# Cross-attention with routed experts: the q product in two halves, in two PSUM banks

## The chip, the cores and the metric

One core of one Trainium2 chip. The metric is the device time of one execution of the kernel in microseconds, the median of several runs. TensorE (PE in the profile) multiplies, VectorE (DVE) and ScalarE (ACT) work on what it leaves in PSUM, GpSimd (POOL) works on SBUF alone, and SyncE (SP) issues most of the transfers. Each engine works through its own instructions in order and waits on semaphores.

## What is computed

The input `x` is 8 batches of 512 tokens of width 512 in float32; with it comes a context of 64 tokens of width 128 for each batch. One layer is computed:

```python
x = x + xattn(layernorm(x), ctx, Wq, Wkv_expand, Wout)
x = x + ffn(layernorm(x), router_w, wg, wu, wd, sg_w, ..., sd_b)

# xattn: 16 heads of 32, a causal mask over the 64 keys
qp = q @ Wq.T
k, v = split(ctx @ Wkv_expand.T)
scores = where(causal, qh @ kh.T / sqrt(32), finfo.min)
out = softmax(scores) @ vh @ Wout.T

# ffn: top 2 of 8 experts by logit (the logit is the weight), and a shared expert
moe = sum over the chosen e of logit[e] * (silu(x @ wg[e]) * (x @ wu[e])) @ wd[e]
out = moe + (silu(x @ sg_w + sg_b) * (x @ su_w + su_b)) @ sd_w + sd_b
```

## The kernel before, in words

A float32 operand of a product is held as two float16 parts, high and low, and a product is three float16 passes (high by high, high by low, low by high; `PASSES`). So every result of PE that feeds another product is read twice out of PSUM: ACT writes the high part (`copy`, L665), and DVE writes what is left as the low part (`low`, L808; L934 for the attention output).

The work has two stages. **The attention stage** takes the 4096 tokens in 32 tiles of 128 (`over_tiles`, L297, calls `step(b, j)` with tile = 4b + j; four tiles make a batch). It is a software pipeline: step `tile` does a different part for each of the tiles t1 = tile - 1 to t5 = tile - 5. **The expert stage** (`entry(n)`) does the shared expert for the 32 tiles and then 71 slots of routed tokens, and begins in the last steps of the attention stage.

What one step does on each engine, in the order in which the engine has it:

- PE (L1276): the q product of t2, 48 matmuls into bank 5 (`turned`, L1267, in the order of the four blocks of 128 output rows); transposes of the attention output of t4 (bank 4), of the probabilities of t3 (banks 0 and 1), of the second norm of t5 (bank 6), and of the first norm `xn1` of t1 (bank 7, L1302 to L1305); the scores of t2 (L1318, 12 matmuls, after a wait for `qT_ready`, into banks 2 and 3); the output projection of t4; the attention product of t3; the router product of t5.
- ACT (L697): logits of t6, the second norm of t5 (L707), the high part of q of t2 (L711), the high parts of attnT, probsT (two), xn2T and xn1T (L725), and in step (0, 2) alone `more_weights` (L727: the high parts of `w_o`, `w_sh`, `w_r`); then the first norm of `tile` (L730), pieces of an expert's weights, and the exponential (L738).
- DVE (L918): the statistics of the first norm of `tile`, a maximum over a third of an expert's weights (L895, not where j = 1), the low part of q of t2 (L929), in step (0, 2) the low part of `w_o` (L931, it waits for `wo_hi` from ACT), the low parts of attnT, probsT (two), xn2T and xn1T, the maximum and the subtraction of the softmax (L955 to L961, L955 where j = 2), the residual (L969) and its statistics, and the attention output (L977, L980). Step (0, 2) ends with `shared_weights`.
- POOL (L558): the power for both norms (L524 to L530), the low parts of the expert's pieces, and where j = 1 four copies of the batch's keys (L545).

`q_mm`, `qT_hi` and `qT_ready` count tiles: one signal of PE, ACT and DVE for each q product. The product of t2 waits for `xn1T_ready` (which also says that bank 7 has been read) and for `qT_ready` of the tile before.

In step (0, 2) PE has one more thing in its order ahead of the transposes of `xn1`: `spread_magnitudes`, which makes the scales of the remaining weights. The weights' high parts on ACT wait for `scales_ready` and stand behind the xn1T copy of that step in ACT's order.

Of the kernel before, what the change touches and what calls it, by code (L numbers as in the profile page):

```python
# [32 lines left out]
P = 128  # L33
B, S, H = 8, 512, 512
# [46 lines left out]
def xattn_moe(nc, x, ctxT, wqT, wkT, wvT, woT, routerT, experts, shared, sh_b, sd_b, out):  # L81
# [5 lines left out]
    with stack:  # L87
# [125 lines left out]
            probsT_flat[:, 0:8 * P], probsT_flat[:, 8 * P:16 * P])]  # L213
        GATE_BANK, UP_BANK, DOWN_BANK, XG_BANK, RANK_BANK, HOT_BANK = (5, 7), (2, 3), (0, 1), (4, 6), 4, 6
        GU_BANK, HT_BANK = GATE_BANK, UP_BANK
        y = w_q[:, :, :].rearrange("p v w -> p (v w)").bitcast(F32).rearrange("p (r w) -> p r w", r=Y_RING)
        attn_flat = attn[:, :, :].rearrange("p h d -> p (h d)")
        y_w = sb("y_w", [P, 4, 1])
# [7 lines left out]
        def flat(t4):  # L226
            return t4.rearrange("p c q -> p (c q)")
# [128 lines left out]
        def _(sp):  # L356
# [55 lines left out]
            def load_shared(n):  # L412

                if n >= 4:
                    sp.wait_ge(up_mm, n - 3)
                else:
                    sp.wait_ge((q_mm, scores_mm, av_mm, av_mm)[n], T)
                sp.wait_ge(xT_stored, 16 * (n + 1))
                sp.dma_start(xgT[n % 4].rearrange("p v c q -> p (v c q)"), xT_dram[n * P:(n + 1) * P, :]
                             ).then_inc(shared_in[n % 4], 16)  # L420
# [242 lines left out]
        def _(act):  # L663
# [33 lines left out]
            def step(b, j):  # L697
                tile = TPB * b + j
                t1, t2, t3, t4, t5, t6 = [tile - n for n in range(1, 7)]
                e, pieces = pieces_at(b, j)  # L700
                if live(t6):
                    act.wait_ge(router_mm, t6 + 1)
                    copy(logits[:, bass.ds(t6, 1), :], psum[:, 6, 0:E], sc[:, S_R:S_R + 1], logits_ready)
                if live(t5):
                    act.wait_ge(ln_rstd[1], t5 + 1)
                    wait(act, xn2_stored[(j + 1) % 2], 16 * (TPB // 2 * b + (j - 5) // 2))
                    act.activation(xn2[:, (j + 1) % 2, 0:H], x1, ACT.Identity, bias=rstd[:, 1, 2:3],  # L707
                                   scale=rstd[:, 1, 1:2]).then_inc(xn2_ready, 1)
                if live(t2):
                    act.wait_ge(q_mm, t2 + 1)  # L710
                    copy(flat(qT[:, 0, :, :]), bank(5), Q_DOWN, qT_hi)  # L711
                if live(t4):
                    act.wait_ge(attnT_mm, t4 + 1)
                    copy(flat(attnT[:, 0, :, :]), bank(4), 1.0, attnT_hi)
                if live(t3):
                    for n in range(2):
                        act.wait_ge(probsT_mm, 2 * t3 + n + 1)
                        copy(probsT_flat[:, 4 * P * n:4 * P * n + 4 * P], bank(n), P_UP, probsT_hi)
                if live(t5):
                    act.wait_ge(xn2T_mm, t5 + 1)  # L720
                    wait(act, xT_stored, 16 * t5)
                    copy(flat(xn2T[:, 0, :, :]), bank(6), X_UP, xn2T_hi)
                if live(t1):
                    act.wait_ge(xn1T_mm, t1 + 1)
                    copy(flat(xn1T[:, 0, :, :]), bank(7), X_UP, xn1T_hi)  # L725
                if isinstance(b, int) and (b, j) == (0, 2):
                    more_weights()  # L727
                if live(tile):
                    act.wait_ge(ln_rstd[0], tile + 1)
                    act.activation(xn1[:, :], x_in[:, j % 2, 0:H], ACT.Identity, bias=rstd[:, 0, 2:3],  # L730
                                   scale=rstd[:, 0, 1:2]).then_inc(xn1_ready, 1)
                if pieces:
                    high_piece(e, pieces[0])
                entry_amid(tile, entry)
                if live(t2):

                    act.wait_ge(shifted, t2 + 1)
                    act.activation(probs[:, :, :], probs[:, :, :], ACT.Exp, scale=sc[:, S_EXP:S_EXP + 1]).then_inc(probs_ready, 1)  # L738
                if len(pieces) > 1:
                    high_piece(e, pieces[1])  # L740
                if isinstance(b, int) and (b, j) == (0, 0):
                    first_weights()
# [34 lines left out]
        def _(dve):  # L777
# [140 lines left out]
            def step(b, j):  # L918
# [6 lines left out]
                if e is not None and j in ((1, 2, 3) if isinstance(b, int) and b == 0 else (0, 2, 3)):  # L925
                    expert_magnitudes(e, max(0, j - 1))
                if live(t2):
                    dve.wait_ge(qT_hi, t2 + 1)
                    low(flat(qT[:, 1, :, :]), bank(5), Q_DOWN, flat(qT[:, 0, :, :]), qT_ready)  # L929
                if isinstance(b, int) and (b, j) == (0, 2):  # L930
                    more_weights()  # L931
                if live(t4):
# [279 lines left out]
        def _(pe):  # L1212
# [63 lines left out]
            def step(b, j):  # L1276
                tile = TPB * b + j
                t1, t2, t3, t4, t5 = [tile - n for n in range(1, 6)]
                if live(t2):

                    pe.wait_ge(xn1T_ready, t2 + 1)
                    wait(pe, qT_ready, t2)
                    if isinstance(t2, int) and t2 == 0:
                        pe.wait_ge(wq_split, 1)
                    turned(bank(5), xn1T, lambda v, c, o: w_q[:, v, c * H + o * P:c * H + (o + 1) * P], C, q_mm)
                if isinstance(b, int) and (b, j) == (0, 2):
                    spread_magnitudes(M_WO, N_MAG)
                if live(t4):
                    pe.wait_ge(attn_ready, t4 + 1)
                    wait(pe, x1_ready, t4)  # L1290
                    transposes(bank(4), attn_flat, C, attnT_mm)
                if live(t3):

                    pe.wait_ge(probs_ready, t3 + 1)
                    wait(pe, attn_ready, t3)
                    for n in range(2):
                        transposes(bank(n), probs_flat[:, 4 * P * n:4 * P * n + 4 * P], PAIRS // 2, probsT_mm)
                if live(t5):
                    pe.wait_ge(xn2_ready, t5 + 1)
                    wait(pe, logits_ready, t5)  # L1300
                    transposes(bank(6), xn2[:, (j + 1) % 2, :], C, xn2T_mm)
                if live(t1):  # L1302
                    pe.wait_ge(xn1_ready, t1 + 1)
                    wait(pe, xn1T_ready, t1)
                    transposes(bank(7), xn1[:, :], C, xn1T_mm)  # L1305
                entry_amid(tile, entry)
                if live(t2):

                    pe.wait_ge(qT_ready, t2 + 1)
                    if isinstance(t2, int) and t2 == 0:  # L1310
                        pe.wait_ge(v_split, 4)
                    wait(pe, shifted, t2)
                    if j == 2:
                        pe.wait_ge(k_bd_ready, HPC * (b + 1))
                    for c in range(C):
                        dst = psum[:, 2 + c // 2, (c % 2) * 2 * P:(c % 2) * 2 * P + 2 * P]
                        for a, z in PASSES:
                            last = pe.matmul(dst, qT[:, a, c, :], k_bd[:, z, c, :, :].rearrange("p h k -> p (h k)"),  # L1318
                                             start=(a == z == 0), stop=(a == 1))
                    last.then_inc(scores_mm, 1)  # L1320
                if live(t4):
                    pe.wait_ge(attnT_ready, t4 + 1)
                    if isinstance(t4, int) and t4 == 0:
                        pe.wait_ge(wo_split, 1)
                    product(bank(4), chunks(attnT), columns(w_o, H), C, proj_mm)
                if live(t3):

                    pe.wait_ge(probsT_ready, 2 * (t3 + 1))
                    if j == 3:
                        pe.wait_ge(v_bd_ready, 2 * (b + 1))  # L1330
                    for r in range(PAIRS):
                        dst = psum[:, r // 4, (r % 4) * 2 * VW:(r % 4 + 1) * 2 * VW]
                        for a, z in PASSES:
                            last = pe.matmul(dst, probsT[:, a, r, :], v_bd[:, z, r, :, :].rearrange("p h w -> p (h w)"),
                                             start=(a == z == 0), stop=(a == 1))
                    last.then_inc(av_mm, 1)
                if live(t5):

                    pe.wait_ge(xn2T_ready, t5 + 1)
                    if isinstance(t5, int) and t5 == 0:  # L1340
                        pe.wait_ge(wsh_split, 3)
                    product(psum[:, 6, 0:E], chunks(xn2T), columns(w_r, E), C, router_mm)
                if isinstance(b, int) and (b, j) == (0, 0):
                    first_products()
# [116 lines left out]
```

## Time and profile before

| | |
|---|---|
| median of 3 runs | 892.38 us |
| the three runs | 892.25, 892.38, 895.52 us |
| the profiled execution, its own time | 895.16 us |
| its span from the first to the last instruction | 893.0 us |
| mean granted TensorE clock | 0.976 |
| busy: PE, DVE, ACT, POOL | 89%, 74%, 46%, 43% of the span |
| chain that ended last | PE 46%, DVE 30%, issue 12%, POOL 5%, ACT 3% |
| attention stage | to about 420 us |

The shares are averages over both stages: PE is what the expert stage runs at, from about 450 us on, and DVE is busiest in the attention stage. The 2.2 us between span and time lie outside the first and last instruction.

### The profile page before, as it was taken

What the parts mean: (1) busy time and instruction counts of PE and PEld (TensorE: products, weight loads), DVE (VectorE), ACT (ScalarE), POOL (GpSimd) and SP (SyncE); (2) the same over time, 40 slices, a digit from 0 to 9 for tenths busy, and PEclk for the clock granted to TensorE, in tenths of its full rate; (3) what the DMA queues carried; (4) which work ended last, traced back from release to release, by engine and by line L of the source; (5) the groups of instructions that cost most, each with busy time, mean ns of one, the idle gap of its engine ahead of it and who ended that gap; (6) DMA issues with size and microseconds to landing.
All of it is one profiled execution on the core that took longest, in us unless ns stands there. A gap on an engine that the chain in (4) does not pass through costs nothing.

```text
span 893.0 us, 22190 instructions
## 1 busy us (share of the span) xinstructions
PE 798.8 (89%) x7484; PEld 541.0 (61%) x7484; DVE 660.2 (74%) x1352; ACT 408.5 (46%) x737; POOL 380.5 (43%) x486
## 2 busy tenths in 40 slices
PE   4559888888898999898999889999999999999994
PEld 1347666767676767676788667645555555555551
DVE  4899999999999999988547887755555555555552
ACT  2345757666666666675532222333333333333330
POOL 1113546454554555553400001046656556656543
PEclk9779999999999999999999999999999999999997
DMA  8215373636363544333576456479989989999892
GB/s 315 97 29 171 107 211 102 192 106 199 104 197 107 164 148 119 105 104 125 185 248 191 143 160 209 135 110 167 147 141 156 148 144 162 148 160 140 147 149 38
DMA packets 102760, 132.39 MB, mean 148 GB/s; under 512 B 54368, under 2 KB 55392, under 8 KB 101280
## 3 DMA queue, kind: packets, MB, share of 16 engines
q1 hardware_dynamic: 86784, 95.74, 37.9%
q0 software_dynamic: 15904, 35.70, 23.2%
q8 instruction: 44, 0.72, 0.4%
q14 instruction: 28, 0.23, 0.1%
HBM read 71.61 MB, written 52.31 MB: 139 GB/s over the span
## 4 chain that ended last, share of the span: by engine, by line
PE 46%; DVE 30%; issue 12%; POOL 5%; ACT 3%; DMA 2%; DVEq 1%; POOLq 1%; SPq 0%; ACTq 0%; another core or an unknown queue 0%
PE psum L1224 33%; PE psum L1272 7%; PE psum L1215 4%; DVE stats L883 4%; DVE head_max L959 3%; DVE probsT L808 3%; DVE xy L969 2%; POOL kv_store L545 2%; DVE xn1T L808 2%; DVE emag L895 1%; DVE qT L808 1%; DMA hidT<-hid_parts 1%; POOL rstd L526 1%; DVE attnT L934 1%; DVE probs L955 1%
## 5 line engine op out<-in xcount | busy, mean ns | idle before, releaser
L645 POOL DMA_INDIRECT out<-w_q,tabs x71 | 112.5, 1584 | 108.7 <-DVE w_q L1203 76.2
L635 POOL DMA_INDIRECT x_in<-normed_tokens,tabs x71 | 71.0, 999 | 147.3 <-DVE tabs L1090 101.1
L1188 DVE SCALAR_TENSOR_TENSOR hid<-psum,tabs,silu_g 128x256 f32<-128x256 f32 x71 | 34.4, 484 | 110.4 <-ACT silu_g L770 108.9
L1224 PE MATMUL psum<-exp_all,hidT 128*128 x426 | 104.5, 382 | 3.2 <-DMA hidT<-hid_parts 3.2
L770 ACT ACTIVATE silu_g<-psum,tabs 128x256 f32<-128x256 f32 x71 | 33.7, 474 | 145.2 <-PE psum L1224 141.1
L1272 PE MATMUL psum<-xn1T,w_q 128*128 128x128 f16 x1536 | 92.6, 221 | 7.5 <-DVE xn1T L808 7.3
L1224 PE MATMUL psum<-exp_all,probsT 128*128 x420 | 96.4, 379 | 0.0
L1272 PEld LDWEIGHTS psum<-xn1T,w_q 128*128 128x128 f16 x1536 | 87.6, 99 | 8.4 <-DVE xn1T L808 8.2
L1224 PE MATMUL psum<-w_o,attnT 128*128 128x512 f16 x384 | 88.9, 381 | 0.0
L524 POOL TENSOR_SCALAR rstd<-moments 128x1 f32<-128x1 f32 x64 | 14.3, 223 | 174.6 <-DVE moments L886 170.8
L738 ACT ACTIVATE probs<-probs,sc 128x1024 f32<-128x1024 f32 x32 | 36.8, 1149 | 84.6 <-DVE probs L961 84.6
L537 POOL TENSOR_TENSOR exp_all<-piece,exp_all 128x512 f32 (+1 forms) x48 | 56.1, 1168 | 44.4 <-ACT piece L665 44.4
L1224 PEld LDWEIGHTS psum<-exp_all,hidT 128*128 128x128 f16 x426 | 41.8, 98 | 54.5 <-issue 5.8
L1318 PE MATMUL psum<-kv_store,qT 128*128 128x256 f16 x384 | 50.5, 284 | 25.4 <-DVE qT L808 24.4
L1203 DVE TENSOR_SCALAR w_q<-psum,y_w 128x512 f32<-128x512 f32 x71 | 53.3, 751 | 22.1 <-PE psum L1224 17.5
L1224 PEld LDWEIGHTS psum<-exp_all,probsT 128*128 128x128 f16 x420 | 41.1, 98 | 41.9
L808 DVE SCALAR_TENSOR_TENSOR probsT<-psum,probsT 128x512 f16<-128x512 f32 x99 | 65.1, 684 | 0.2 <-ACT probsT L665 0.2
L1224 PEld LDWEIGHTS psum<-w_o,attnT 128*128 128x128 f16 x384 | 37.8, 99 | 39.4 <-issue 1.1
L1318 PEld LDWEIGHTS psum<-kv_store,qT 128*128 128x128 f16 x384 | 36.2, 101 | 37.9 <-DVE qT L808 30.6
L665 ACT ACTIVATE probsT<-psum 128x512 f16<-128x512 f32 x99 | 55.6, 599 | 8.0 <-PE psum L1215 7.7
L1224 PE MATMUL psum<-exp_all,xn1T 128*128 x216 | 49.6, 379 | 0.0
L1224 PE MATMUL psum<-exp_all,qT 128*128 x216 | 49.6, 379 | 0.0
(195 smaller groups left out, 1646.1 us busy)
## 6 DMA issues: line engine op xcount, KB each, us to landing
x_in<-x SPq DMA_DIRECT2D x64, 256.0 KB, 2.9
exp_all<-experts SPq DMA_DIRECT2D x8, 1536.0 KB, 7.3
out<-xy SPq DMA_DIRECT2D x32, 256.0 KB, 2.0
normed_tokens<-xn SPq DMA_DIRECT2D x32, 256.0 KB, 2.1
normed_turned<-xn2T SPq DMA_DIRECT2D x32, 256.0 KB, 2.0
w_q<-out SPq DMA_DIRECT2D x32, 256.0 KB, 2.9
out<-w_q SPq DMA_DIRECT2D x32, 256.0 KB, 2.4
probsT<-normed_turned SPq DMA_DIRECT2D x16, 256.0 KB, 3.5
```

The source lines that it names most:

```text
L537: pool.tensor_tensor(split_piece(e, 1, k), piece[:, :], split_piece(e, 0, k), ALU.subtract).then_inc(piece_split, 1)
L635: pool.indirect_dma_start(x_in[:, t % 4, :], None, xn_dram, bass.IndirectOffsetOnAxis(gather_at[:, t:t + 1], 0)).then_inc(gathered[t % 4], 16)
L645: pool.indirect_dma_start(out, bass.IndirectOffsetOnAxis(add_at[:, t:t + 1], 0), y[:, t % Y_RING, :], None, bounds_check=TOKENS - 1, oob_i ...
L665: act.activation(dst, src, ACT.Copy, scale=scale).then_inc(done, 1)
L738: act.activation(probs[:, :, :], probs[:, :, :], ACT.Exp, scale=sc[:, S_EXP:S_EXP + 1]).then_inc(probs_ready, 1)
L808: dve.scalar_tensor_tensor(dst, src, scale, high, ALU.mult, ALU.subtract).then_inc(done, 1)
L883: dve.bn_stats(stats[:, which, :], src).then_inc(ln_chain[which], 1)
L1203: dve.tensor_scalar(y[:, k % Y_RING, :], bank(DOWN_BANK[k % 2]), y_w[:, tk % 4, :], None, ALU.mult).then_inc(y_ready, 1)
L1215: last = pe.transpose(dst[:, c * P:(c + 1) * P], src[:, c * P:(c + 1) * P], ident[:, :])
L1224: last = pe.matmul(dst, lhsT(a, c), rhs(z, c), start=(c == 0 and a == z == 0), stop=(c == n - 1 and a == 1))
L1272: last = pe.matmul(dst[:, o * P:(o + 1) * P], weights(a, c, o), xT[:, z, c, :], start=(c == 0 and a == z == 0), stop=(c == C - 1 and a == 1))
L1318: last = pe.matmul(dst, qT[:, a, c, :], k_bd[:, z, c, :, :].rearrange("p h k -> p (h k)"), start=(a == z == 0), stop=(a == 1))
```

## The change

The q product of a tile is made in two halves of 24 matmuls: output blocks 0 and 1 go to columns 0 to 255 of bank 5, and blocks 2 and 3 to columns 256 to 511 of bank 7. Each half has its own signal, and ACT and DVE each make two instructions of 128x256 where they made one of 128x512. All waits on the three semaphores count halves. Bank 7 is also the bank of the xn1 transposes, so these now wait until DVE has taken the second half (`qT_ready` at 2 * t2 + 2). The scores wait for the first half ahead of chunk 0 and for the second half ahead of chunk 2; they stand behind the xn1 transposes in PE's order as before.

```diff
+        Q_BANKS = (5, 7)
...
-                    sp.wait_ge((q_mm, scores_mm, av_mm, av_mm)[n], T)
+                    sp.wait_ge((q_mm, scores_mm, av_mm, av_mm)[n], (2 * T, T, T, T)[n])
...
                 if live(t2):
-                    act.wait_ge(q_mm, t2 + 1)
-                    copy(flat(qT[:, 0, :, :]), bank(5), Q_DOWN, qT_hi)
+                    for n in range(2):
+                        act.wait_ge(q_mm, 2 * t2 + n + 1)
+                        copy(flat(qT[:, 0, 2 * n:2 * n + 2, :]), psum[:, Q_BANKS[n], 2 * P * n:2 * P * n + 2 * P], Q_DOWN, qT_hi)
...
                 if live(t2):
-                    dve.wait_ge(qT_hi, t2 + 1)
-                    low(flat(qT[:, 1, :, :]), bank(5), Q_DOWN, flat(qT[:, 0, :, :]), qT_ready)
+                    for n in range(2):
+                        dve.wait_ge(qT_hi, 2 * t2 + n + 1)
+                        low(flat(qT[:, 1, 2 * n:2 * n + 2, :]), psum[:, Q_BANKS[n], 2 * P * n:2 * P * n + 2 * P], Q_DOWN,
+                            flat(qT[:, 0, 2 * n:2 * n + 2, :]), qT_ready)
...
-                    wait(pe, qT_ready, t2)
+                    wait(pe, qT_ready, 2 * t2)
                     if isinstance(t2, int) and t2 == 0:
                         pe.wait_ge(wq_split, 1)
-                    turned(bank(5), xn1T, lambda v, c, o: w_q[:, v, c * H + o * P:c * H + (o + 1) * P], C, q_mm)
+                    for n in range(2):
+                        turned(psum[:, Q_BANKS[n], 2 * P * n:2 * P * n + 2 * P], xn1T,
+                               lambda v, c, o: w_q[:, v, c * H + (2 * n + o) * P:c * H + (2 * n + o + 1) * P], C // 2, q_mm)
...
                 if live(t1):
                     pe.wait_ge(xn1_ready, t1 + 1)
                     wait(pe, xn1T_ready, t1)
+                    if live(t2):
+                        pe.wait_ge(qT_ready, 2 * t2 + 2)
                     transposes(bank(7), xn1[:, :], C, xn1T_mm)
                 entry_amid(tile, entry)
                 if live(t2):
 
-                    pe.wait_ge(qT_ready, t2 + 1)
+                    pe.wait_ge(qT_ready, 2 * t2 + 1)
...
                     for c in range(C):
+                        if c == 2:
+                            pe.wait_ge(qT_ready, 2 * t2 + 2)
                         dst = psum[:, 2 + c // 2, (c % 2) * 2 * P:(c % 2) * 2 * P + 2 * P]
```

## Rows read from the trace of the kernel before

**Rows 1.** Busy time of each engine (x instructions) in two stretches, granted clock, DMA

```profile
100.00:396.00 296.00, 262.34 (x3208) 206.58 (x3206) 275.07 (x438) 193.78 (x328) 150.27 (x251) 0.99 0.45 140
...
600.00:700.00 100.00, 99.76 (x508) 51.28 (x507) 56.39 (x137) 33.92 (x69) 59.44 (x47) 1.00 0.94 152
```

**Rows 2.** Waits, whole trace: engine, line, releaser: us in total, times, longest

```profile
PE psum L1318 <- DVE qT L808: 24.4, 23, 5.4
...
DVE qT L808 <- ACT qT L665: 7.4, 9, 2.1
```

**Rows 3.** Timeline of DVE, a step with j = 2: start, us, instruction, [idle before]

```profile
281.80 0.69 DVE L808 SCALAR_TENSOR_TENSOR qT<-psum,qT 128x512 f16<-128x512 f32 x1 [0.87 <-ACT qT L665]
282.40 0.68 DVE L934 TENSOR_TENSOR attnT<-psum,attnT 128x512 f16<-128x512 f32 x1
283.00 1.28 DVE L808 SCALAR_TENSOR_TENSOR probsT<-psum,probsT 128x512 f16<-128x512 f32 x2
```

**Rows 4.** Timeline of ACT, the same step

```profile
280.47 0.81 ACT L707 ACTIVATE xn<-xy,rstd 128x512 f32<-128x512 f32 x1 [1.79 <-POOL rstd L530]
281.19 0.58 ACT L665 ACTIVATE qT<-psum 128x512 f16<-128x512 f32 x1
...
281.66 0.59 ACT L665 ACTIVATE attnT<-psum 128x512 f16<-128x512 f32 x1
```

**Rows 5.** Timeline of DVE and PE, a step with j = 3

```profile
246.60 0.69 DVE L808 SCALAR_TENSOR_TENSOR qT<-psum,qT 128x512 f16<-128x512 f32 x1
...
247.34 1.49 PE L1318 MATMUL psum<-kv_store,qT 128*128 128x256 f16 x12
...
248.66 2.75 PE L1224 MATMUL psum<-w_o,attnT 128*128 128x512 f16 x12
...
250.19 1.21 DVE L959 TENSOR_REDUCE head_max<-psum 128x16 f32<-128x1024 f32 x1
...
252.58 0.74 DVE L969 SCALAR_TENSOR_TENSOR xy<-psum,sc,x_in 128x512 f32<-128x512 f32 x1
```

**Rows 6.** Timeline of DVE, step (0, 2)

```profile
48.47 0.68 DVE L808 SCALAR_TENSOR_TENSOR qT<-psum,qT 128x512 f16<-128x512 f32 x1
49.07 2.34 DVE L808 SCALAR_TENSOR_TENSOR w_o<-exp_all,inv,w_o 128x2048 f16<-128x2048 f32 x1
```

**Rows 7.** Timeline of ACT, step (0, 2)

```profile
43.81 0.60 ACT L665 ACTIVATE xn1T<-psum 128x512 f16<-128x512 f32 x1 [3.32 <-PE psum L1215]
46.56 2.00 ACT L665 ACTIVATE w_o<-exp_all,inv 128x2048 f16<-128x2048 f32 x1 [2.15 <-DVE inv L868]
```

**Rows 8.** Timeline of PE, steps (0, 2) and (0, 3)

```profile
42.66 1.11 PE L1215 MATMUL psum<-ident,xn 128*128 128x128 f32 x4
49.21 2.74 PE L1318 MATMUL psum<-kv_store,qT 128*128 128x256 f16 x12 [5.44 <-DVE qT L808]
...
57.89 0.60 PE L1215 MATMUL psum<-ident,xn 128*128 128x128 f32 x4
62.10 2.40 PE L1318 MATMUL psum<-kv_store,qT 128*128 128x256 f16 x12 [3.60 <-DVE qT L808]
```

**Rows 9.** Busy time in a stretch of step (0, 2), columns as in rows 1

```profile
49.00:52.00 3.00, 2.74 (x12) 1.64 (x12) 3.00 (x4) 3.00 (x4) 0.00 (x0) 0.50 0.00 0
```

**Rows 10.** Timeline of DVE, step (0, 3)

```profile
61.36 0.68 DVE L808 SCALAR_TENSOR_TENSOR qT<-psum,qT 128x512 f16<-128x512 f32 x1
...
64.54 1.23 DVE L959 TENSOR_REDUCE head_max<-psum 128x16 f32<-128x1024 f32 x1 [0.70 <-PE psum L1318]
```

**Rows 11.** DVE instructions of other widths: timeline, and one line's durations (min/median/max ns)

```profile
274.89 1.22 DVE L961 TENSOR_TENSOR probs<-psum,head_max 128x1024 f32<-128x1024 f32 x1
276.03 0.74 DVE L969 SCALAR_TENSOR_TENSOR xy<-psum,sc,x_in 128x512 f32<-128x512 f32 x1
...
425.26 0.61 DVE L1179 SCALAR_TENSOR_TENSOR hid<-psum,sh_bias,silu_g 128x128 f32<-128x128 f32 x2 [2.32 <-ACT silu_g L760]
...
L1179 DVE SCALAR_TENSOR_TENSOR hid<-psum,sh_bias,silu_g x64: 334/343/352, 425.3 to 570.1; 128x128 f32<-128x128 f32 x64
```

## The prediction

> **What bounds the kernel now.** The first view is the busy time by stretches. In the steady part of the attention stage DVE works 275.07 of 296.00 us (93%), PE 262.34; in the routed part of the expert stage PE works 99.76 of 100.00 [rows 1]. So the attention stage is DVE's and the expert stage PE's. The expert stage is not touched and starts when the attention stage lets it, so what the change costs or saves on DVE before 420 us moves the end by as much.
>
> The second view is who waited for whom. PE waited 24.4 us in 23 waits for q's low part, ahead of the scores. That is the wait that the change aims at, but PE isn't the bound there. What counts is DVE's own wait for q's high part: 7.4 us in 9 waits, 2.1 the longest [rows 2].
>
> The third view is the timeline of single steps. DVE runs its list without a gap except where j = 2: there it waits 0.87 us for ACT [rows 3], and ACT's q copy starts at 281.19 not because PE is late but because it stands behind the second norm, which waited for POOL [rows 4]. With j = 3 (and 0) the scores leave slack: they end at 248.83 and DVE needs them at 250.19; the output projection ends at 251.41 and DVE needs it at 252.58 [rows 5].
>
> **The change, part by part.**
>
> *The split on DVE.* One instruction becomes two. Back to back, starts of 512-wide instructions lie 0.60 us apart (281.80, 282.40, 283.00 in [rows 3]), those of a 1024-wide one and the next 1.14 (274.89 to 276.03 in [rows 11]). So 512 more columns cost 0.54, each instruction 0.06 beside its columns, and a half 0.33: the split costs DVE 2 x 0.33 - 0.60 = 0.06 us a tile. The dearest reading is the 128-wide pair of L1179: 0.61 for both less 0.34 for the last is 0.27 from start to start [rows 11], less 0.135 for its columns, so 0.13; it reads other operands, so I take 0.06 and keep 0.13 as upper end. The lower end is 0: the columns must be read anyway, no row shows a gain from splitting.
>
> This is the price on which a rule bears. The row shows 0.06 on PSUM input. The Trainium skill (Perfetto Trace Analysis, "Optimizing Scalar/DVE Operations") says that a DVE instruction on PSUM carries about 125 ns beside its data and that larger operations pay where the engine is saturated; by that figure, as an estimate, the part of the steady steps below would be about 1.4 us and not 0.4. The same section says that breaking up instructions may help where ACT and DVE aren't saturated but hold up others; here DVE is the busy one, so that condition isn't met.
>
> *Where DVE waits, j = 2.* ACT's half copy ends about half of its 0.47 pitch earlier (281.19 to 281.66 in [rows 4]), so 0.23: DVE can start at 281.57 and would be done with both halves by the next start at 282.23. But ACT too has one instruction more, of which no row shows the price: its bounds are 0 and DVE's 0.13, and I take 0.05. Then ACT's attnT copy begins at 281.71 and ends at 282.30, and DVE's attnT low part starts at about 282.34, not 282.40. Gain 0.06 a batch; bounds 0.23 (nothing else is late) and nothing. The wait is not removed, it is handed to attnT's copy.
>
> *Steady steps.* Per batch: +0.06 with j = 3, +0.06 with j = 0, -0.06 with j = 2, and with j = 1 nothing, since DVE arrives early at the wait of the next step, whose chain (POOL's key copies, the second norm) doesn't pass q. That is +0.06, times 7 batches +0.4 us. Bounds: 0.13 twice and no gain, 0.26 x 7 = +1.8; and 0 with the whole 0.23, -1.6.
>
> *The xn1 transposes behind q's low part.* In a steady step they now start when the second half is done, at about 247.41 (0.73 to 0.74 after q's start at 246.60 as now, and 0.06 more), and the four at full clock take 0.60 at most [rows 8], so the scores start at about 248.0 instead of 247.34 and end at 249.5: before 250.19. The projection ends at 252.1, before 252.58. What is queued behind the waiting transposes on PE is the rest of the step, some 0.6 us later; it is covered by slack of 0.7 and 0.5. If that cover were gone, it would cost up to 0.1 to 0.6 a tile.
>
> *The same wait in step (0, 2): the term that decides.* Now the xn1 transposes run at 42.66, long before q's low part at 48.47; ACT turns them into xn1T's high part at 43.81 and is free for the weights' high parts, `w_o` at 46.56 [rows 6, 7, 8]. DVE takes the low part of `w_o` at 49.07, 0.51 after ACT has ended it at 48.56. After the change PE may transpose only when DVE has both halves of q: 48.47 + 0.33 + 0.41 (0.68 less the 0.27 of the columns left out) = 49.21, and with the 0.06 from DVE's end to PE's start (49.15 to 49.21) at 49.27. At the lower of its two clock levels, 1.2 GHz, which the stretch behind PE's idle time shows (0.50, [rows 9]), the four transposes take 1.11 as at 42.66 [rows 8]: 50.38. ACT's xn1T copy starts 0.04 later at 50.42, the `w_o` copy one pitch of a 512-wide copy (0.47 in [rows 4]) behind it at 50.9, and ends 2.00 later [rows 7], at 52.9. DVE, which stands at the wait for `wo_hi` with everything else queued behind it, starts at about 52.93 instead of 49.07: **+3.9 us**, on the bounding engine, in DVE's unbroken list. The scores of this step would end about 53.1 (50.38 + 2.74) and DVE asks for them only behind the low parts of `w_o` (2.34) and xn1T (0.6), at 55.9, so they add nothing. Bounds: 3.3 if the transposes went at full clock (0.60), 4.1 if ACT's steps are slower than taken.
>
> *The same wait in step (0, 3).* The transposes at 57.89 were done before PE fell idle; now they stand between q's low part (61.36, done 62.10) and the scores. DVE already waits 0.70 there for the scores to end at 64.50 [rows 10]. It waits longer by the transposes' length: 0.60 to 1.11 [rows 8], and 0.06 for the split; the scores could also lose up to 0.34 (2.74 against 2.40) if the clock is at the lower level throughout. I take **+1.0**; bounds 0.6 and 1.5.
>
> *The rest.* Waits of SP (q_mm at 2T) come to the same moment. The last two tiles: the 2.1 us wait shrinks by the same 0.06. The expert stage sees no new instruction. PE's matmuls are the same 48 in the same order.
>
> **Sum:** 3.9 + 1.0 + 0.4 = +5.3 us. The profiled execution took 895.16 us (span 893.0), 2.8 over the median, so the sum gives 900.5 for an execution like it, and 892.4 + 5.3 = **897.7** for the median. A measurement of this kernel can tell about 0.5% from no change, 4.5 us: the line lies at 896.9.
>
> **Rivals.**
>
> *The start-up loss is in part made good (about +2.9, 895.3).* If ACT's weights' copies need not wait (or the chain through POOL in batch 1 is the later one whatever DVE does), part of the 4.9 is taken up by a wait of DVE that shrinks. For it: DVE has waits, 7.4 us in all [rows 2]. Against it: those with j = 2 start from DVE's own statistics a step earlier and so move with DVE. It decides if the stretch from 48 to 56 us is no longer than now plus 2. The price: half of 4.9 kept, 2.5, and the 0.4.
>
> *It is faster.* One mechanism: DVE's wait for q's high part, 7.4 us in 9 waits [rows 2], goes altogether, since half the copy is there before DVE comes. Without the start-up loss that gives 892.4 - 7.4 = 885.0, with it 889.9. It decides where ACT would have the first half before 280.9, the time at which DVE is free (281.80 less 0.87); but ACT has its second norm until 281.28 [rows 3, 4], so I give it little.
>
> *Slower still (about +8.9, 901.3).* PE's delay of 0.6 in steady steps isn't covered in the steps with j = 0 or 3, and 0.1 to 0.2 us reaches DVE in some 24 tiles (+3.6) on top of the 5.3. For it: PE works 89% of that stage and the projection has only 0.5 left. Against: 250.19 and 252.58 are met as worked out. It decides if DVE shows idle time ahead of L959 or L969 in steady steps.
>
> That the halves do nothing useful for PE's scores (they stand behind transposes that need the second half anyway) is part of the forecast: their wait for the first half can never be the last one, except in the step without t1.
>
> **How the numbers follow.** The forecast case (+4.5 to +6.5) has 0.62, the smaller loss 0.26, slower still 0.08, faster 0.04. The forecast case lies above the line of +4.5 nearly whole, and slower still does: 0.68 for slower, once a little is taken from and given to either side. Faster by over 0.5% is 0.03, for the rest of that case lands within. Within 0.5%: 0.29. The range goes down past the smaller loss's centre to 894 (a few of the cheap ends of the sum), and up past the dear ends (4.1 + 1.5 + 1.8 = 7.4) to slower still's centre, 901.5.
>
> **What the profile would show.** Right: ACT's xn1T copy of step (0, 2) behind 50 us and not at 43.8; DVE idle 3 to 4 us ahead of `w_o`, released by ACT; about 1.7 us idle ahead of L959 in step (0, 3); L808 on q as pairs 0.33 apart; a batch as long as now within 0.1 us, read from one batch's L969 to the next's. The prediction is wrong if `w_o` still starts near 49, if a batch takes over 0.3 us more or less than now, or if the steps with j = 2 lose their wait without a new one ahead of attnT.

## The result

The changed kernel is **slower: 903.09 us** (median of 4 runs, 901.76 to 905.36) against 893.76 us (median of 4, 892.25 to 895.52). The ratio is 1.0106, 95% interval 1.0074 to 1.0138: +9.5 us, with 6.6 to 12.3 inside the interval. Predicted were +5.3 us and 897.7, with a range up to 901.5. The direction was right; the time lies above the range.

### The profile after

The page of the changed kernel. PE's busy time is as before within a microsecond (798.8 us before), ACT's too (408.5), and DVE's is 3.7 us longer (660.2 before); DVE and ACT have 32 instructions more.

```profile
span 901.1 us, 22296 instructions
PE 798.0 (89%) x7484; PEld 545.2 (61%) x7484; DVE 663.9 (74%) x1384; ACT 409.3 (45%) x769; POOL 379.4 (42%) x486
```

So the greater part of the loss is idle time, and the first question is where. Timeline of DVE in steps (0, 2) and (0, 3), against [rows 6, 10]:

```profile
45.38 0.75 DVE L810 SCALAR_TENSOR_TENSOR qT<-psum,qT 128x256 f16<-128x256 f32 x2
50.00 2.35 DVE L810 SCALAR_TENSOR_TENSOR w_o<-exp_all,inv,w_o 128x2048 f16<-128x2048 f32 x1 [3.87 <-ACT w_o L666]
...
64.88 0.69 DVE L810 SCALAR_TENSOR_TENSOR xn1T<-psum,xn1T 128x512 f16<-128x512 f32 x1 [0.70 <-ACT xn1T L666]
66.65 1.22 DVE L963 TENSOR_REDUCE head_max<-psum 128x16 f32<-128x1024 f32 x1 [1.08 <-PE psum L1328]
```

ACT and PE in the same steps, against [rows 7, 8]:

```profile
47.40 0.60 ACT L666 ACTIVATE xn1T<-psum 128x512 f16<-128x512 f32 x1 [10.17 <-PE psum L1219]
47.89 1.99 ACT L666 ACTIVATE w_o<-exp_all,inv 128x2048 f16<-128x2048 f32 x1
```

```profile
46.28 1.09 PE L1219 MATMUL psum<-ident,xn 128*128 128x128 f32 x4 [6.63 <-DVE qT L810]
47.16 2.50 PE L1328 MATMUL psum<-kv_store,qT 128*128 128x256 f16 x12
...
63.13 1.08 PE L1219 MATMUL psum<-ident,xn 128*128 128x128 f32 x4 [4.19 <-DVE qT L810]
64.01 2.61 PE L1328 MATMUL psum<-kv_store,qT 128*128 128x256 f16 x12
```

This is the chain that the prediction named: q's low part, transposes (1.09 us, slow), xn1T copy, `w_o` copy, and DVE idle 3.87 us. In step (0, 3) DVE now waits 0.70 + 1.08 = 1.78 us where it had waited 0.70.

The steady part is the second place. The DVE instruction that applies the mask comes once a batch. First in the kernel before (batches 1, 2 and 7), then in the changed one (batches 1 to 7):

```profile
96.27 1.21 DVE L955 TENSOR_TENSOR probs<-psum,mask 128x1024 f32<-128x1024 f32 x1
143.46 1.22 DVE L955 TENSOR_TENSOR probs<-psum,mask 128x1024 f32<-128x1024 f32 x1
...
379.96 1.22 DVE L955 TENSOR_TENSOR probs<-psum,mask 128x1024 f32<-128x1024 f32 x1
```

```profile
98.72 1.22 DVE L959 TENSOR_TENSOR probs<-psum,mask 128x1024 f32<-128x1024 f32 x1
146.67 1.22 DVE L959 TENSOR_TENSOR probs<-psum,mask 128x1024 f32<-128x1024 f32 x1
194.32 1.22 DVE L959 TENSOR_TENSOR probs<-psum,mask 128x1024 f32<-128x1024 f32 x1
242.40 1.22 DVE L959 TENSOR_TENSOR probs<-psum,mask 128x1024 f32<-128x1024 f32 x1
290.02 1.22 DVE L959 TENSOR_TENSOR probs<-psum,mask 128x1024 f32<-128x1024 f32 x1
337.63 1.22 DVE L959 TENSOR_TENSOR probs<-psum,mask 128x1024 f32<-128x1024 f32 x1
385.69 1.22 DVE L959 TENSOR_TENSOR probs<-psum,mask 128x1024 f32<-128x1024 f32 x1
```

Before, six batches took 283.69 us, 47.28 each. After, they took 286.97: three took 47.61 to 47.65 (call them plain), and three 47.95, 48.08 and 48.06. That is +3.3 us, where the prediction had 0.06 a batch.

What is different where j = 1? First the kernel before (PE's scores, ACT, and POOL's last step of the power):

```profile
270.79 1.48 PE L1318 MATMUL psum<-kv_store,qT 128*128 128x256 f16 x12 [1.67 <-DVE qT L808]
```

```profile
270.27 0.62 ACT L665 ACTIVATE xn1T<-psum 128x512 f16<-128x512 f32 x1
271.78 0.81 ACT L730 ACTIVATE xn<-x_in,rstd 128x512 f32<-128x512 f32 x1 [0.88 <-POOL rstd L530]
```

```profile
271.47 0.27 POOL L530 TENSOR_SCALAR rstd<-moments,rstd 128x1 f32<-128x1 f32 x1 [0.21 <-POOL rstd L526]
```

Then a plain batch of the changed kernel, in the same order:

```profile
322.90 0.66 PE L1219 MATMUL psum<-ident,xn 128*128 128x128 f32 x4 [2.23 <-DVE qT L810]
```

```profile
323.60 0.60 ACT L666 ACTIVATE xn1T<-psum 128x512 f16<-128x512 f32 x1 [1.14 <-PE psum L1219]
324.09 0.80 ACT L732 ACTIVATE xn<-x_in,rstd 128x512 f32<-128x512 f32 x1
324.80 0.71 ACT L666 ACTIVATE exp_all<-exp_all,esc  x1
```

```profile
323.46 0.26 POOL L531 TENSOR_SCALAR rstd<-moments,rstd 128x1 f32<-128x1 f32 x1 [0.21 <-POOL rstd L527]
```

ACT's xn1T copy waits 1.14 us for the transposes. Before, ACT's first norm started 0.04 us after POOL's power; now POOL is done at 323.72 and the norm starts at 324.09, behind the xn1T copy, 0.33 us later than it could. Behind it stands the high part of a piece of an expert's weights, which starts the chain through POOL that ends in the wait of the next step, j = 2.

In the longer batches PE's clock falls at that same place. PE, and the granted clock around it (the last three columns are the clock, the DMA share and GB/s):

```profile
131.46 1.11 PE L1219 MATMUL psum<-ident,xn 128*128 128x128 f32 x4 [2.22 <-DVE qT L810]
132.37 2.56 PE L1328 MATMUL psum<-kv_store,qT 128*128 128x256 f16 x12
```

```profile
133.00:134.00 1.00, 1.00 (x7) 0.74 (x5) 1.00 (x3) 1.00 (x3) 0.00 (x0) 0.50 0.00 0
```

```profile
134.97 1.23 DVE L963 TENSOR_REDUCE head_max<-psum 128x16 f32<-128x1024 f32 x1 [0.57 <-PE psum L1328]
```

PE is idle for 2.22 us, comes back at 0.50 of its clock (1.2 GHz), and the transposes and scores take 3.5 us in place of about 2.0; DVE then waits 0.57 us for the scores. The falls differ from trace to trace, and the idle time ahead of them is as long in batches without one.

### The profile page after: what moved, and what is told of

Same layout as the page of the kernel before. It is cut to its first block, busy times and chain, and to the rows that moved or that the text cites. A ratio compares the mean times of both kernels' runs of the same rounds, so it can differ in the third digit from the quotient of the medians.

```text
span 901.1 us, 22296 instructions
## 1 busy us (share of the span) xinstructions
PE 798.0 (89%) x7484; PEld 545.2 (61%) x7484; DVE 663.9 (74%) x1384; ACT 409.3 (45%) x769; POOL 379.4 (42%) x486
## 4 chain that ended last, share of the span: by engine, by line
PE 46%; DVE 30%; issue 11%; POOL 4%; ACT 4%; DMA 3%; DVEq 1%; POOLq 0%; SPq 0%; ACTq 0%; another core or an unknown queue 0%
PE psum L1228 32%; PE psum L1276 7%; PE psum L1219 5%; DVE stats L885 4%; DVE head_max L963 3%; DVE probsT L810 3%; DVE qT L810 2%; DVE xy L973 2%; POOL kv_store L546 2%; DMA hidT<-hid_parts 2%; DVE xn1T L810 2%; DVE attnT L938 1%; DVE probs L959 1%; DVE emax L912 1%; POOL exp_all L538 1%
## 5 line engine op out<-in xcount | busy, mean ns | idle before, releaser
L1219 PE MATMUL psum<-ident,xn 128*128 128x128 f32 x256 | 44.4, 299 | 46.2 <-DVE qT L810 39.3
L1219 PEld LDWEIGHTS psum<-ident,xn 128*128 128x128 f32 x256 | 28.9, 148 | 61.0 <-DVE qT L810 29.3
L1328 PE MATMUL psum<-kv_store,qT 128*128 128x256 f16 x384 | 52.4, 292 | 0.7 <-DVE qT L810 0.7
```

Of the source, the lines that this page charges most:

```text
L1219: last = pe.transpose(dst[:, c * P:(c + 1) * P], src[:, c * P:(c + 1) * P], ident[:, :])
```

## The experiments

Totals of different traces can't be compared to a microsecond: the stretch before step (0, 2) ends anywhere from 42 to 47 us. So besides the ratio, two stretches of the profiled executions and their sum are given: **start-up**, from the statistics of step (0, 2) to the mask of batch 1; **six batches**, from there to the mask of batch 7; and their sum, against the kernel before (49.91 + 283.69 = 333.60).

| kernel | start-up | six batches | sum against before | ratio to before, 95% interval |
|---|---|---|---|---|
| before | 49.91 | 283.69 | | |
| changed | 55.45 | 286.97 | +8.8 | 1.0106 (1.0074 to 1.0138) |
| e1, split alone | 49.37 | 285.60 | +1.4 | 1.0022 (0.9994 to 1.005) |
| e2, wait alone | 55.33 | 286.92 | +8.7 | 1.0098 (1.0064 to 1.0132) |
| e3, w_o first | 52.68 | 286.95 | +6.0 | 1.0067 (1.0047 to 1.0087) |
| e4, banks swapped | 54.60 | 284.24 | +5.2 | 1.0053 (1.0026 to 1.008) |
| e5, both | 51.72 | 284.81 | +2.9 | 1.0025 (1.0004 to 1.0045) |
| e8, PE kept busy | 55.20 | 285.51 | +7.1 | 1.0081 (1.0056 to 1.0106) |
| e11, high part early | 54.50 | 283.51 | +4.4 | 1.0044 (1.0022 to 1.0066) |
| e9, repairs and order | 51.23 | 283.28 | +0.9 | 1.0023 (0.9996 to 1.0049) |
| e6, q before the norm | 49.69 | 281.28 | -2.6 | 0.9957 (0.9935 to 0.9979) |
| e7, q and attnT | 48.56 | 281.12 | -3.9 | 0.9974 (0.9953 to 0.9995) |
| e12, before, high early | 49.71 | 278.89 | -5.0 | 0.9921 (0.989 to 0.9951) |
| e13, e6 and e12 | 49.33 | 278.08 | -6.2 | 0.9906 (0.9881 to 0.9931) |

The two right-hand columns follow each other within 2.3 us (1% is 8.9 us), and the expert stage that follows took 472 to 475 us in every trace in which its start is marked by the same wait. So the loss is in these two stretches.

**e1: the split without the wait.** The edit is shown against the changed kernel.

```diff
-                        act.wait_ge(q_mm, 2 * t2 + n + 1)
+                        act.wait_ge(q_mm, t2 + 1)
...
-                        dve.wait_ge(qT_hi, 2 * t2 + n + 1)
+                        dve.wait_ge(qT_hi, 2 * t2 + 2)
...
-                    if live(t2):
-                        pe.wait_ge(qT_ready, 2 * t2 + 2)
                     transposes(bank(7), xn1[:, :], C, xn1T_mm)
```

(and the product whole in bank 5 with one signal.)

> ACT and DVE take q in two halves, but PE makes the whole product in bank 5 with one signal, DVE waits for both of ACT's halves, and the xn1 transposes don't wait for q's low part. Theory (the wait of the xn1 transposes is the cost): only the instructions' own price is left, 0.06 us a tile on DVE and 0.05 more in ACT's chain where j = 2, so 0.1 to 0.3 us a batch; +1 to +2.5 us against the kernel before, w_o's low part on DVE begins without an idle time ahead of it, and a batch takes 47.4 to 47.6 us (47.28 before). Rival (more instructions and signals are the cost): +6 us or more, a batch over 47.8.

+2.0 us by the ratio, within noise of none; start-up lost nothing and a batch took 47.60. Theory held. The split itself costs 0.32 us a batch here, where DVE gets no earlier start from it: that is nearly as much as a plain batch of the changed kernel lost, so how the two kinds of cost go together has to be worked out (below).

**e2: the wait without the split,** in the kernel before.

```diff
                     wait(pe, xn1T_ready, t1)
+                    if live(t2):
+                        pe.wait_ge(qT_ready, t2 + 1)
                     transposes(bank(7), xn1[:, :], C, xn1T_mm)
```

> The kernel before, q whole in bank 5, with one wait added: the xn1 transposes wait for q's low part. Theory: start-up loses what it lost in the changed kernel, 3.8 us ahead of w_o and 1.0 in the next step, and each batch 0.27 us or so through ACT's xn1T copy where j = 1, plus 0.4 in those batches in which PE's clock falls after its idle time; together +6.5 to +9 us against before. Rival (splitting is the cost, the wait is covered by slack): +0 to +1.5 us.

One wait reproduces the changed kernel: +8.8 us by the ratio, start-up 55.33 against 55.45, and DVE's waits of start-up are nearly the same (3.87, 1.08 and 0.70 in the changed kernel):

```profile
DVE w_o L808 <- ACT w_o L665: 3.9, 1, 3.9
DVE head_max L959 <- PE psum L1320: 1.2, 1, 1.2
...
DVE xn1T L808 <- ACT xn1T L665: 0.7, 1, 0.7
```

Its two plain batches took 47.53 and 47.52 (+0.25), four with a fall of the clock 47.88 to 48.05.

**e3: the start-up wait taken away by ACT's order,** in the changed kernel. `w_o` is split off `more_weights` and goes ahead.

```diff
+                if isinstance(b, int) and (b, j) == (0, 2):
+                    out_weights()
                 if live(t1):
                     act.wait_ge(xn1T_mm, t1 + 1)
```

> The changed kernel, but in step (0, 2) ACT makes w_o's high part ahead of its xn1T copy. Theory: DVE's idle time of 3.87 us ahead of w_o's low part goes, nothing else changes: 3.5 to 4 us faster than the changed kernel, +5 to +6 us against before. Rival (the start of w_o is not on the path, or DVE waits for xn1T in its stead): within 1 us of the changed kernel.

Start-up gained 2.77 us, not 3.87: the wait for `w_o` is gone, a new one comes after it (0.97 us), and the one of the next step is 1.20 us instead of 1.08. DVE in step (0, 2):

```profile
45.12 2.34 DVE L814 SCALAR_TENSOR_TENSOR w_o<-exp_all,inv,w_o 128x2048 f16<-128x2048 f32 x1
47.38 0.68 DVE L814 SCALAR_TENSOR_TENSOR xn1T<-psum,xn1T 128x512 f16<-128x512 f32 x1
49.03 1.23 DVE L963 TENSOR_TENSOR probs<-psum,mask 128x1024 f32<-128x1024 f32 x1 [0.97 <-PE psum L1332]
```

The scores, 1.1 us late behind the slow transposes, had been hidden by the wait for `w_o`; now they come last, 0.97 us. The expectation (3.5 to 4) missed by that; by the ratios the gain is 3.5.

**e4: the halves change banks,** so that the xn1 transposes need the first half alone.

```diff
-        Q_BANKS = (5, 7)
+        Q_BANKS = (7, 5)
...
-                        pe.wait_ge(qT_ready, 2 * t2 + 2)
+                        pe.wait_ge(qT_ready, 2 * t2 + 1)
                     transposes(bank(7), xn1[:, :], C, xn1T_mm)
```

> The changed kernel with the banks the other way: the first half of q goes to bank 7 and the second to bank 5, so the xn1 transposes wait for the first half alone. Theory: they start 0.33 us earlier in every step, so ACT's xn1T copy where j = 1 isn't late: a batch takes 47.3 to 47.45 us in place of 47.6, and start-up loses 0.3 less twice; 2.5 to 3.5 us faster than the changed kernel, +5 to +7 against before, with DVE still idle 3.5 us ahead of w_o. Rival (the batch is longer by the split itself, not by the transposes' start): 0.7 us faster or less, a batch still 47.6.

3.6 us less than the changed kernel in the two stretches and 4.7 by the ratios, a little more than the 2.5 to 3.5 expected. DVE's idle time ahead of `w_o` was 3.54 us. Batches took 47.18 to 47.32 but for two, 47.65 and 47.50, and where j = 1 ACT waits 0.81 us for the transposes instead of 1.14:

```profile
322.61 0.60 ACT L666 ACTIVATE xn1T<-psum 128x512 f16<-128x512 f32 x1 [0.81 <-PE psum L1219]
```

**e5: e3 and e4 together.**

> The changed kernel with both repairs: banks swapped (the xn1 transposes wait for the first half alone) and w_o's high part ahead of the xn1T copy on ACT in step (0, 2). Theory: costs add up, so the 2.8 us that the second repair gave by itself come on top of the first's 3.6: +2 to +3 us against the kernel before; from the statistics of step (0, 2) to the mask of batch 1 about 51.8 us (49.9 before), a batch 47.3 to 47.4. Rival (both repairs take away the same wait): +4.5 us or more.

The two add: 2.9 us are left over the kernel before in the two stretches, 2.2 by the ratio. Start-up was as expected, but three of the six batches took 47.56 to 47.71, each with a fall of PE's clock. With both repairs the halves cost still.

**e8: is it the idle time that lets the clock fall?** Twelve transposes of the identity are added on PE in the changed kernel.

```diff
                     if live(t2):
+                        if j == 1:
+                            wait(pe, shifted, t2)
+                            for _ in range(12):
+                                pe.transpose(psum[:, 2, 0:P], ident[:, :], ident[:, :])
                         pe.wait_ge(qT_ready, 2 * t2 + 2)
```

> The changed kernel with 12 transposes of the identity added on PE where j = 1, into bank 2, ahead of the wait for q's low part; their results are written over. Theory (in half the batches PE's clock falls in the idle time of 2.2 us that the wait opens, and each fall costs 0.43 us): the idle time is under 1 us, the granted clock stays at 1.00 from 100 us on, every batch takes 47.6 us, 1 to 1.5 us faster than the changed kernel. Rival (the falls have nothing to do with that idle time, or cost nothing): falls in the same places, 286.9 us for six batches as in the changed kernel.

In this trace, yes. PE where j = 1, and the granted clock behind it:

```profile
128.64 1.47 PE L1315 MATMUL psum<-ident 128*128 128x128 f32 x12
131.02 0.66 PE L1219 MATMUL psum<-ident,xn 128*128 128x128 f32 x4 [0.91 <-DVE qT L810]
131.51 1.47 PE L1332 MATMUL psum<-kv_store,qT 128*128 128x256 f16 x12
```

```profile
131.00:133.00 2.00, 1.98 (x17) 1.76 (x18) 2.00 (x4) 1.29 (x3) 0.63 (x2) 1.00 0.00 0
```

The clock was 1.00 in every stretch of 50 us from 100 to 400, and all six batches took 47.50 to 47.62. Work that nobody needs made the six batches 1.46 us shorter; by the ratios the gain over the changed kernel is 2.2 us, with intervals that overlap. The run shortens the idle time and adds work at once and doesn't tell these two apart. That no fall came by chance is unlikely: with idle times of 2.2 us 14 of 24 batches had one (the changed kernel, e2, e3, e11). By the Trainium skill (Perfetto Trace Analysis, "Matmul Optimizations") the matmul engine scales its power with its utilization and should be given its work back to back; this run agrees, 0.91 us of idle time against 2.22.

**e11: is the batch's loss the chain through ACT's xn1T copy?** In the changed kernel, where j = 1, the high part of the piece goes ahead of that copy.

```diff
+                if pieces and j == 1:
+                    high_piece(e, pieces[0])
                 if live(t1):
                     act.wait_ge(xn1T_mm, t1 + 1)
...
-                if pieces:
+                if pieces and j != 1:
                     high_piece(e, pieces[0])
```

> The changed kernel, but where j = 1 ACT makes the first high part of an expert's piece ahead of its xn1T copy and not behind the first norm. Theory (the wait where j = 2 comes from the chain xn1 transposes, ACT's xn1T copy, high part, POOL): the chain starts 1.5 us earlier or more and no longer hangs on q's low part, DVE's wait of 0.8 us where j = 2 goes, a batch 46.8 to 47.0 us, 4 to 6 us faster than the changed kernel. Rival (the wait where j = 2 comes from elsewhere, DVE's statistics by themselves): a batch 47.5 us or more.

DVE's wait for q where j = 2 is gone in all six batches. Two batches took 46.61 and 46.57, one us less than plain ones of the changed kernel. The four others took 47.48 to 47.62: there the clock falls, and without the wait of j = 2 nothing takes the delay up; DVE waits for the output projection (L1230), 2.9 us in four times:

```profile
DVE xy L975 <- PE psum L1230: 2.9, 4, 1.0
```

A fall costs 1.0 us here, where DVE has no other wait to lose, and 0.4 in the changed kernel, where it has one. The whole was 5.5 us faster than the changed kernel by the ratios and 4.4 in the two stretches.

**e6, e7: the kernel before, ACT's q copy (e7: and its attnT copy) ahead of the second norm.** DVE's wait where j = 2 was never for PE: ACT had q in front of it and stood at the norm.

```diff
+                if live(t2):
+                    act.wait_ge(q_mm, t2 + 1)
+                    copy(flat(qT[:, 0, :, :]), bank(5), Q_DOWN, qT_hi)
                 if live(t5):
                     act.wait_ge(ln_rstd[1], t5 + 1)
...
-                if live(t2):
-                    act.wait_ge(q_mm, t2 + 1)
-                    copy(flat(qT[:, 0, :, :]), bank(5), Q_DOWN, qT_hi)
```

> The kernel before, with ACT's q copy moved ahead of its second norm. Theory: where j = 2, ACT is idle while it waits for POOL's power though q has long been there; DVE's wait of 0.87 us for q's high part goes, and a smaller one comes ahead of attnT's low part, whose copy still stands behind the norm; 0.6 us a batch, 4 to 5 us faster than before with the last tiles. Rival (the second norm is delayed and the xn2 and xn1 transposes with it): no gain or a loss.

> The kernel before, with ACT's q and attnT copies both moved ahead of its second norm. Theory: the whole wait of 0.87 us a batch goes, a batch takes 46.4 to 46.5 us, and the last tiles gain 1 to 2 us; 6 to 8 us faster than before. Rival: with j = 0 the norm comes 0.4 us later and what hangs on it (xn2 and xn1 transposes) reaches DVE: less gain than with the q copy alone.

e6 is 3.8 us faster than the kernel before, a little under the 4 to 5 expected. Of e7 6 to 8 us were expected, and the ratio gives 2.3. Its interval overlaps that of e6, and its two stretches are 1.3 us shorter than e6's, so which of the two is faster is open. In its trace ACT waits for the attention transposes ahead of the norm (0.30 us where j = 3). Why it isn't faster was not followed further.

**e9: the halves on top of both repairs and e6's order.**

> The changed kernel with banks swapped, w_o's high part first, and ACT's two q copies ahead of its second norm. Theory (DVE bounds the stage; once its wait for q is gone in another way, the halves have nothing left to give and cost their 0.06 a tile): 1 to 3 us slower than the kernel before with the order alone (e6_q_before_norm), -2 to +0.5 us against before, a batch 47.0 to 47.2 us. Rival (the halves still help through an earlier start): as fast as e6_q_before_norm or faster, a batch 46.9 or less.

+2.1 us against before and 5.9 against e6, more than expected: start-up 1.5 us longer than in e6, six batches 2.0. Part of the 2.0 is the clock: four of its six batches had a fall, two of e6's. The two without one took 46.73 and 47.02 us, those of e6 46.60 to 46.93. With DVE's wait for q gone in another way, nothing speaks for the halves.

**e12, e13: e11's move in the kernel before, alone and with e6's.**

> The kernel before with the same move of the high part where j = 1. Theory: DVE's wait of 0.87 us where j = 2 goes, a batch takes 46.4 to 46.5 us, 5 to 6.5 us faster than before. Rival (ACT's xn1T copy, 1.4 us later, reaches DVE's xn1T low part): 46.9 us a batch or more.

> The kernel before with that move and the q copy ahead of the second norm. Theory: both take away the same wait, so a batch is that of the one alone, 46.4 us, and only the last tiles gain 1 us more; 5.5 to 7.5 us faster than before. Rival (they add): 8 us faster or more.

**Both beat both kernels:** e12 887.73 us, 7.1 us less than before by the ratio, and e13 886.48 us, 8.4 less. The mask of e12, batches 4 to 6, 46.30 us apart:

```profile
235.89 1.21 DVE L957 TENSOR_TENSOR probs<-psum,mask 128x1024 f32<-128x1024 f32 x1
282.19 1.21 DVE L957 TENSOR_TENSOR probs<-psum,mask 128x1024 f32<-128x1024 f32 x1
328.49 1.21 DVE L957 TENSOR_TENSOR probs<-psum,mask 128x1024 f32<-128x1024 f32 x1
```

Three batches of the two runs had a fall of the clock and took 46.74 and 46.87 (e12) and 46.93 (e13), 0.4 to 0.7 us more than the others. There too DVE has no wait for q where j = 2 to lose, so the 1.0 of e11 is not the price of every such fall; in e11 PE has the transposes behind q's low part as well, which may be why.

The intervals of e12 and e13 overlap, so whether e6's order adds anything to the early high part isn't settled.

## Why the prediction was right and wrong

**What held.** The stage is DVE's, and what matters is DVE's idle time. The term that was to decide did: ahead of `w_o` 3.9 us were predicted and 3.87 measured, and in step (0, 3) DVE's idle time grew by 1.08 for a predicted 1.0. e2 shows that the one wait ahead of the xn1 transposes causes both. The pair of DVE halves takes 0.66 us from its start to the next instruction (298.48 to 299.14), the 0.06 more that were worked out from [rows 3, 11]. The 125 ns for each instruction of the Trainium skill (Perfetto Trace Analysis, "Optimizing Scalar/DVE Operations") would have made it 2 x (0.27 + 0.125) = 0.79 as an estimate; the trace doesn't show that. In j = 2 the gain was handed to attnT's copy as said: DVE's first half began 0.21 us earlier against ACT's norm (1.12 us behind its start, 1.33 before), and its next instruction starts at once when ACT's attnT copy ends:

```profile
286.26 0.76 DVE L810 SCALAR_TENSOR_TENSOR qT<-psum,qT 128x256 f16<-128x256 f32 x2 [0.83 <-ACT qT L666]
287.02 0.69 DVE L938 TENSOR_TENSOR attnT<-psum,attnT 128x512 f16<-128x512 f32 x1
```

**The step that failed** is "with j = 1 nothing, since DVE arrives early at the wait of the next step, whose chain (POOL's key copies, the second norm) doesn't pass q". The chain does: it begins on ACT, with the high part of a piece that stands behind the xn1T copy, and that copy waits for transposes which the change puts behind q's low part. The prediction followed the delayed transposes to the scores and the projection on PE and to DVE's xn1T low part, found 0.7 and 0.5 us of slack, and did not follow them through ACT's queue. It did so for step (0, 2), where the same queue holds `w_o`, and not for the steady step, where it holds the piece. In the trace of before the xn1T copy starts 1.47 us ahead of the end of POOL's power (270.27 against 271.74) and ACT then idles 0.88 us; in the changed kernel it starts 0.12 us ahead (323.60 against 323.72). That is 1.35 us later. The slack, from the copy's start to the norm's less the 0.49 from one start to the next, is 271.78 - 270.27 - 0.49 = 1.02 us, and the rest is the 0.33. The views of before would have shown it: q's low part is there at 270.79, and with the prediction's own 0.06, 0.60, 0.04 and 0.47 behind it the norm comes at 271.96 and not at 271.78.

The sizes: a plain batch of the changed kernel costs 0.34 us more (mean of 47.65, 47.62, 47.61 less 47.28). The wait alone costs 0.25 (e2) and the split alone 0.32 (e1); the two together would be 0.57. Of the missing 0.23, 0.18 is what the early first half gives back where j = 2: attnT's low part starts 1.93 us behind ACT's norm in the kernel before (280.47 to 282.40), 2.06 in e1 (326.82 to 328.88) and 1.88 in the changed kernel (285.14 to 287.02). So the prediction's +0.06, +0.06 and -0.06 held (-0.05 was read), and the 0.33 where j = 1 is what it lacked; together these are 0.40, for the measured 0.34. By its own sign, a batch over 0.3 us longer, it was wrong: 47.83 on average against 47.28. Swapping the banks (e4) takes the delay down to where it and the gain cancel, about 47.3. That DVE's wait where j = 2 hangs on the piece behind ACT's xn1T copy is shown by e11, which leaves the wait on PE as it is and takes only the piece out from behind the copy. The same move gains about as much in the kernel before (e12, 47.28 to 46.3), so that the change delays this chain is shown by e2 and e4 and not by e11.

**The second miss is the clock.** The prediction had PE's delay covered in each steady step and put no price on PE's clock beyond start-up. The wait makes PE's idle time where j = 1 2.2 us long (1.67 us before), the clock fell behind it in three of six batches, and each fall cost about 0.4 us, 1.2 together. e8, without a fall, agrees with both. In the kernel before one stretch of 50 us has such a fall as well (0.97 from 300 to 350 us) and its batch took 47.29. It cost nothing there: DVE waited 0.47 us for the output projection, and its wait for q where j = 2, 0.87 us in most batches, was 0.31:

```profile
323.87 0.75 DVE L969 SCALAR_TENSOR_TENSOR xy<-psum,sc,x_in 128x512 f32<-128x512 f32 x1 [0.47 <-PE psum L1224]
...
329.08 0.69 DVE L808 SCALAR_TENSOR_TENSOR qT<-psum,qT 128x512 f16<-128x512 f32 x1 [0.31 <-ACT qT L665]
```

The rival "slower still" had this form, DVE idle ahead of the scores' maximum in steady steps, but placed it in steps with j = 0 or 3 and for another reason.

**The sum.** Start-up +5.5 us (predicted 4.9 and the first steps' 0.1), six batches +3.3 (predicted 0.4): +8.8 in the profiled executions and +9.5 by the ratio. The start-up part missed by 0.5. Counted from the statistics of step (0, 2), DVE is 3.96 us later at the end of that step (3.9 predicted), 1.24 more at the scores' maximum of step (0, 3) (1.0 predicted), and 0.34 more at the mask of batch 1 (0.1 predicted), of which 0.06, 0.07 and 0.15 come at the three pairs of q.

Two smaller readings were off and move little. DVE's list has another gap in each batch than that of j = 2, 0.26 us ahead of its maximum over the weights. And the wait of 2.08 us of the last tiles shrank to 1.86, by 0.22 and not by 0.06.

**The rivals.** "Faster" had DVE's wait for q going altogether: it went from 0.87 to 0.83. "In part made good" is out as well: the stretch that was to decide it grew by 4.0 us, and the stages behind didn't win it back. The median of the kernel before was 892.38 in the 3 runs shown and 893.7 to 894.8 in the later and more numerous ones, so about 1 to 2 us of the distance to 903.09 is the base.

## What to carry to other kernels

A buffer shared by two uses is a wait, and its price stands in every queue behind the one that waits: follow it through each engine that reads the delayed result, to what that engine has next, in the steady step as in the first. Splitting an operation on the busiest engine must save it a wait that is really for the producer; here DVE waited for ACT's order, and moving one or two instructions in that order gave 7 to 8 us where the halves lost 9.5. A start-up step has its own order of work and deserves its own walk through the timeline.

## What the runs showed of the hardware that was not expected

The clock falls on PE last a few microseconds at 0.50 and come at one place, where j = 1. How often they come follows the idle time of PE there, over the traces kept: 14 of 24 batches with 2.2 us (the changed kernel, e2, e3, e11), 11 of 18 with 1.9 (e4, e5, e9), 6 of 24 with 1.67 (the kernel before, e6, e12, e13), one of 12 with 1.3 to 1.5 (e1, e7), and none of 6 with 0.9 (e8, with 1.47 us of useless transposes in the gap). These are few batches for each length. Batches of equal work differed by it, by nothing in the kernel before, by 0.4 us in the changed one and by 1.0 in e11, according to what wait of DVE was there to take the delay up and how far PE was behind already. In the changed kernel the idle time is nearly the same before a fall (2.22 us) and without one (2.23 us), so its length alone doesn't tell which batch is hit.
